# Loading a kernel's weights in three portions behind its first stage, and starting that stage before they are in

## The chip, the cores and the metric

The kernel runs on one core of a Trainium2 chip. The metric is the device time of one execution in microseconds (us). A core has a matrix engine (PE), a vector engine (DVE), an activation engine (ACT, also called ScalarE), a general engine (POOL) and SyncE (SP), which here only issues DMAs and waits. Each engine runs its own list of instructions in order; the lists meet at semaphores. DMAs are issued from ACT and from SP, and 16 DMA engines carry the bytes of both.

## The reference, cut to what matters

`x` has 8 batches of 512 tokens with 128 channels. Eight residual blocks follow each other, each on a layer norm of `x`:

```
x = x + attention_0(norm(x))      # 16 heads of width 8, allowed = block of query >= block of key, others score 0
x = x + fp4_ffn(norm(x))          # weights and activations quantised to 4 bits in blocks of 16
x = x + attention_1(norm(x))      # low-rank terms added to the weights, alibi bias, causal
x = x + ternary_ffn(norm(x))      # four 128..512 wide layers with scales
x = x + attention_2(norm(x))      # full
x = x + rwkv_ffn(norm(x)); x = x + ssm_block(norm(x)); x = x + expert_ffn(norm(x))
```

The first attention, all that the start of the program needs:

```
q, k, v = h @ Wq.T + bq, h @ Wk.T + bk, h @ Wv.T + bv      # h = norm(x)
s = q k' / sqrt(8);  s = 0 where a key's block of 32 comes after the query's
out = softmax(s) v @ Wo.T + bo
```

## The kernel before, in words

All of `x` stays on the core, in `X`, a batch being 512 columns. The stages (the attentions are stages 0, 2 and 4) run one after the other, and in each the 8 batches pass in frames, f = -1 to 8. Frame -1 prepares batches 0 and 1; frame f works on batch f, finishes f - 1 and prepares f + 1. A frame of an attention has 16 slots, s = 0 to 15 (`slots`), and each engine's list is written out by walking over frames and slots, so the code is the order.

**How a batch is prepared.** DVE takes the norm's statistics (`norm_stats`), POOL applies them (`norm_apply`, giving `xn`), PE turns `xn` (`transpose4`) and multiplies by Wq and Wk, ACT copies the results to `qf` and `kf`. Scores are wanted to more than bf16 precision, so `qf` and `kf` are each split into three bf16 parts (`qpart`, `kpart`, four operations; DVE does it for batch 0 of stage 0, POOL for later ones). SP writes the parts to DRAM (`part_out`: six DMAs for q, six for k) and reads them back in another arrangement (`stack`: two DMAs into `Qst`, two into `Kst`), six parts of 8 rows under each other for every head. The rows below the parts hold masks; `load_extra` loads them at the start of a stage, twelve DMAs in stage 0, and SP waits for them before it goes on. A last row of `Qst` is the negated maximum of the scores: PE forms the scores of a batch once to find the maxima (the matmul into banks 4 and 5, `scores`), DVE reduces them, the maxima are turned into `mT`, and SP copies `mT` into `Qst` (two DMAs at slot 6, two at slot 14). Only then are the scores formed transposed, exponentiated by ACT and multiplied by V.

The maxima of the next batch begin at slot 14 of a frame, so that batch's stacks must be in by then. SP's list in a frame: `part_out` of q at slot 5, `mT` at 6, `part_out` of k at 7, both stacks at 8, `mT` at 14. In frame -1 `part_out` of q and the q stack stand together at slot 5.

**How the program starts.** SP issues 8 loads of `X`. ACT issues `first_loads` (14: six constants, and the weights of stage 0's attention) and then `loads` (31, the weights of later stages), and then makes two small operands (`ident_b`, `bq_s`, which count `s_prepared` to 2). PE and DVE set the starting values of the semaphores, half each. `stage_starts` makes every engine, SP among them, wait at stage 0 for `X` of batch 0, POOL's fills, `first_loads` and `s_prepared`; from stage 1 on the engines wait for all of `loads`. The earliest reader of those is the quantiser of the fp4 weights, in frame 7 of stage 0, which has a wait of its own.

Of the kernel before, what the change touches and what calls it, by code (L numbers as in the profile page):

```python
# [143 lines left out]
class Attention(Stage):  # L144
# [161 lines left out]
    def tensor(self, pe):  # L306
        k = self.k
        k.stage_starts(pe, self)
        ps = k.ps

        def ready_t(b, g, tile):
# [108 lines left out]
        def misc_step(f, s):  # L420
# [43 lines left out]
            elif s == 9 and prev.valid():  # L464
# [2 lines left out]
                    pe.wait_ge(self.s_mT.sem, self.s_mT.at(f, 1))  # L467
                context_t(prev, 3)
            elif s == 10 and nxt.valid() and not (self.opened and f.c == -1):
                pe.wait_ge(self.s_cT_read.sem, self.s_cT_read.at(prev))  # L470
                pe.wait_ge(self.s_mT.sem, self.s_mT.at(f, 1))
                pe.wait_ge(self.s_k.sem, self.s_k.at(nxt))
                for t in range(NT):
                    mm = pe.matmul(misc[:, P * t:P * t + P], k.xnT[:, P * t:P * t + P], self.w["v"],
                                   start=True, stop=True)
                mm.then_inc(self.s_v_ps.sem, 1)
            elif s == 11 and prev.valid() and not full:
                pe.wait_ge(self.s_ctx.sem, self.s_ctx.at(prev))
                if nxt.valid():
                    pe.wait_ge(self.s_v.sem, self.s_v.at(nxt))  # L480
                transpose4(k.ctx_rows, self.s_c2_ps)
            elif s == 12 and prev.valid() and not full:
                pe.wait_ge(self.s_c2.sem, self.s_c2.at(prev))
                for t in range(NT):
                    mm = pe.matmul(misc[:, P * t:P * t + P], k.ctxT[:, P * t:P * t + P], self.w["o"],
                                   start=True, stop=True)
                mm.then_inc(self.s_o_ps.sem, 1)
            elif s == 13 and f.valid():
                if nxt.valid():
                    pe.wait_ge(self.s_v.sem, self.s_v.at(nxt))  # L490
                if full:
                    pe.wait_ge(self.s_ctx.sem, self.s_ctx.at(prev))
                else:
                    pe.wait_ge(self.s_x_done.sem, self.s_x_done.at(prev))
                context_t(f, 0)
            elif s == 15 and nxt.valid() and block:

                pe.wait_ge(self.s_mT.sem, self.s_mT.at(f))
                pe.wait_ge(self.s_v.sem, self.s_v.at(nxt))
                if not f.valid():  # L500
                    pe.wait_ge(self.s_k.sem, self.s_k.at(f.plus(2)))
                pe.matmul(misc, k.later[:, :], k.V[:, nxt.par, :, :, 0:DH], start=True, stop=False)
                for jt in range(1, NT):
                    mm = pe.matmul(misc[:, 0:P * jt], k.ones[:, :],
                                   k.V[:, nxt.par, jt, :, 0:DH].unsqueeze(1).broadcast_to([P, jt, H, DH]),
                                   start=False, stop=jt == NT - 1)
                mm.then_inc(self.s_vs_ps.sem, 1)
# [154 lines left out]
    def vector(self, dve):  # L662
        k = self.k
        k.stage_starts(dve, self)
        ps, misc = k.ps, k.ps[:, 7, :]

        def maxima(n, c):
# [70 lines left out]
        def frame(f):  # L738
            prev, nxt = f.plus(-1), f.plus(1)
            for s, _, _, (mb, c) in slots(f):  # L740
# [21 lines left out]
                if s == 9 and prev.valid():  # L762
                    context(prev, 3)
                if s == 10 and nxt.valid() and "bv" in self.w:
                    dve.wait_ge(self.s_v_ps.sem, self.s_v_ps.at(nxt))
                    dve.wait_ge(self.s_pv.sem, self.s_pv.at(nxt.plus(-2)))
                    out = k.V[:, nxt.par, :, :, 0:DH]
# [19 lines left out]
    def gpsimd(self, pool):  # L787
        k = self.k
        k.stage_starts(pool, self)

        def split(n, src, part, at):

# [45 lines left out]
        def frame(f):  # L838
# [25 lines left out]
                context(prev, 3)  # L864
            early(f, 3)
            if block and nxt.valid():
                v = "p (t c) -> p t c"
                x = xs_of(k.X, nxt).rearrange(v, t=NT)
                pool.wait_ge(self.s_cen.sem, self.s_cen.at(nxt))
# [13 lines left out]
    def sync(self, sp):  # L883
        k = self.k
        if self.opened:
            sp.wait_ge(self.s_x_done.sem, self.s_x_done.at(N(None, -1 - NB)))
        else:
            k.stage_starts(sp, self)
        k.load_extra(sp, self)

        def part_out(n, j):
# [29 lines left out]
        def frame(f):  # L921
            nxt = f.plus(1)
            for s in range(16):
                if s in (6, 14) and f.valid():
                    half = (s - 6) // 8
                    sp.wait_ge(self.s_mT.sem, self.s_mT.at(f, half + 1))
                    for a in range(2):
# [1 line left out]
                        sp.dma_start(k.Qst[r:r + 1, f.par, 4 * half:4 * half + 4, :]  # L929
                                     .rearrange("o i (t p) -> o (i t) p", t=NT),  # L930
                                     k.mT[16 * a:16 * a + 16, half, :]).then_inc(self.s_mrow.sem, 16)
                if s in (5, 7) and nxt.valid():
                    part_out(nxt, (s - 5) // 2)
                if s == (5 if f.c == -1 else 8) and nxt.valid():
                    stack(nxt, 0)
                if s == 8 and nxt.valid():
                    stack(nxt, 1)

        frames(sp, frame)


# [1666 lines left out]
class Kernel:  # L2608


    def __init__(self, nc, ctx, dram, out):
# [4 lines left out]
        self.s_fill = self.sem("fill")  # L2616
        self.s_prepared = self.sem("prepared")
        self.s_x_rest = self.sem("x_in_rest")
        self.s_first_weights = self.sem("first_weights")
        self.s_lora = self.sem("lora")  # L2620
        self.s_lora_full = self.sem("lora_full")
# [47 lines left out]
        self.ones = sb("ones", [P, P])  # L2669
        self.ps = ctx.enter_context(nc.psum_tensor("ps", [P, 8, T], F32))  # L2670
        self.scratch = nc.dram_tensor("parts_scratch", (2, 2, NKB, 64, T), BF16, kind="Internal").ap()
        self.first_loads, self.loads = [], []
        self.late_loads = []

        self.late_mem = [self.Qst[:, :, :, :].rearrange("p a h t -> p (a h t)").bitcast(F32),
# [50 lines left out]
    def late_weight(self, name):  # L2726
        src = self.dram[name]
        return self.late(list(src.shape), src)

    def load_late(self, sp, early):  # L2730
        for i, (dst, src) in enumerate(self.late_loads):
            sp.dma_start(dst, src).then_inc(self.s_late if i < early else self.s_later, 16)
# [28 lines left out]
    def const(self, name, dt):  # L2761
        src = self.dram["c_" + name]
        t = self.sb(name, list(src.shape), dt)
        self.first_loads.append((t[:], src))
        return t

    def weight(self, name, shape=None, src=None):

        src = self.dram[name] if src is None else src
        t = self.sb("w_" + name, list(src.shape) if shape is None else shape)  # L2770
        (self.first_loads if name[:4] in ("L0_W", "L0_b") else self.loads).append((t[:], src))
        return t

    def stage_starts(self, eng, st):

        if st.stage == FIRST_STAGE:
            eng.wait_ge(self.s_xin, 16)
            eng.wait_ge(self.s_fill, FILLS)
            eng.wait_ge(self.s_first_weights, 16 * len(self.first_loads))
            eng.wait_ge(self.s_prepared, 2)  # L2780
        else:
            eng.wait_ge(st.s_x_done.sem, st.s_x_done.at(N(None, -1)))
        if st.stage > 0:
            eng.wait_ge(self.s_weights, 16 * len(self.loads))

    def norm_of(self, n, st):

# [84 lines left out]
FILLS = 6  # L2872
# [3 lines left out]
def transformer(nc, dram, out):  # L2876
    with ExitStack() as ctx:
# [35 lines left out]

        @block.scalar
        def _(act):
            for dst, src in k.first_loads:
                act.dma_start(dst, src).then_inc(k.s_first_weights, 16)
            for dst, src in k.loads:
                act.dma_start(dst, src).then_inc(k.s_weights, 16)
            act.wait_ge(k.s_first_weights, 16 * len(k.first_loads))  # L2920
            act.activation(k.ident_b[:, :], k.ident[:, :], ACT.Copy).then_inc(k.s_prepared, 1)
            act.activation(k.bq_s[:, :], k.bq[:, :], ACT.Copy, scale=1.0 / math.sqrt(DH))\
               .then_inc(k.s_prepared, 1)
            for st in stages:
                st.scalar(act)

        @block.vector
        def _(dve):
            for sig in k.starts[1::2]:
                dve.sem_inc(sig.sem, sig.start)  # L2930
            for st in stages:
                st.vector(dve)
# [26 lines left out]
```

## Time and profile before

| | us |
|---|---|
| median of 3 executions | 2198.02 |
| lowest, highest | 2197.54, 2209.73 |
| the profiled execution, span of its instructions | 2200.8 |
| ACT has issued its 45 loads | 23.55 |
| first instruction of the first norm | 25.50 |
| first score matmul of batch 0 | 58.37 |
| slot 14 of frame 0, maxima of batch 1 begin | 99.94 |

For the profiled execution only the span is given, from the first to the last instruction; the median of the times is 2.8 us below it. PE is busy for 83% of the span, DVE 58%, ACT 47%, POOL 32%. In the profile a name like `SPq` or `ACTq` is an engine's instruction queue: its rows show when DMAs are issued, not when their data land. Times of rows are from the start of the span.

### The profile page before, as it was taken

What the parts mean: (1) busy time and instruction counts of PE and PEld (TensorE: products, weight loads), DVE (VectorE), ACT (ScalarE), POOL (GpSimd) and SP (SyncE); (2) the same over time, 40 slices, a digit from 0 to 9 for tenths busy, and PEclk for the clock granted to TensorE, in tenths of its full rate; (3) what the DMA queues carried; (4) which work ended last, traced back from release to release, by engine and by line L of the source; (5) the groups of instructions that cost most, each with busy time, mean ns of one, the idle gap of its engine ahead of it and who ended that gap; (6) DMA issues with size and microseconds to landing.
All of it is one profiled execution on the core that took longest, in us unless ns stands there. A gap on an engine that the chain in (4) does not pass through costs nothing.

```text
span 2200.8 us, 33255 instructions
## 1 busy us (share of the span) xinstructions
PE 1836.4 (83%) x11885; PEld 819.7 (37%) x11885; DVE 1287.4 (58%) x3442; ACT 1045.0 (47%) x1768; POOL 712.4 (32%) x796
## 2 busy tenths in 40 slices
PE   2788787765658888888999999899999957999998
PEld 0233233233433444444444444332332324444443
DVE  1666666627777767773100111598989916676663
ACT  1366556531213655565222322288888854445432
POOL 3166666454542322220100010122232115443330
PEclk9799999867877999998999999799999978999999
DMA  8323343000022343220000002233234110000000
GB/s 198 63 59 66 66 86 74 1 16 1 1 58 59 68 93 74 59 59 3 0 0 1 0 0 58 46 71 59 59 61 85 30 48 1 0 10 5 6 5 15
DMA packets 70269, 91.71 MB, mean 42 GB/s; under 512 B 13228, under 2 KB 63644, under 8 KB 65228
## 3 DMA queue, kind: packets, MB, share of 16 engines
q1 hardware_dynamic: 64680, 84.69, 18.7%
q10 hardware_dynamic: 5424, 4.89, 0.7%
q8 instruction: 95, 1.56, 0.3%
q14 instruction: 70, 0.57, 0.1%
HBM read 49.30 MB, written 39.85 MB: 41 GB/s over the span
## 4 chain that ended last, share of the span: by engine, by line
PE 51%; issue 7%; ACT 5%; DVE 4%; DMA 2%; SPq 1%; POOL 1%; DVEq 0%; ACTq 0%; POOLq 0%
PE ps L1402 9%; PE ps L410 5%; PE ps L2798 3%; PE ps L384 3%; PE ps L368 3%; PE ps L2079 2%; PE ps L396 2%; PE ps L2081 2%; PE ps L2097 2%; PE ps L352 2%; PE ps L330 2%; PE ps L1392 2%; DMA Qst<-mT 2%; PE ps L1772 1%; ACT Pr L579 1%
## 5 line engine op out<-in xcount | busy, mean ns | idle before, releaser
L686 DVE TENSOR_REDUCE mx<-ps 128x1 f32<-128x512 f32 (+3 forms) x1024 | 534.5, 583 | 156.2 <-PE ps L352 124.0
L586 ACT ACTIVATE Pr<-ps 128x1024 f32<-128x1024 f32 (+3 forms) x512 | 348.7, 706 | 229.6 <-PE ps L330 118.8
L579 ACT ACTIVATE Pr<-ps 128x512 f32<-128x512 f32 x512 | 274.6, 602 | 49.0 <-PE ps L384 43.7
L352 PE MATMUL ps<-Kst,Qst 63*128 63x512 bf16 (+3 forms) x1024 | 227.7, 329 | 66.7 <-DVE mx L686 25.6
L330 PE MATMUL ps<-Qst,Kst 64*128 64x512 bf16 (+3 forms) x1024 | 230.7, 328 | 56.0 <-issue 37.0
L682 DVE CUSTOM_DVE_ANT_0 vs<-ps,cT 128x512 f32<-128x512 f32 (+3 forms) x512 | 225.7, 487 | 84.8 <-PE ps L352 81.6
L368 PE MATMUL ps<-Pr,V 128*32 128x512 f32 (+3 forms) x2048 | 207.1, 479 | 4.6 <-ACT ctxU L592 2.9
L396 PE MATMUL ps<-Kst,Qst 63*128 63x512 bf16 x512 | 170.0, 403 | 6.6 <-DVE mx L686 4.4
L410 PE MATMUL ps<-Pr,V 128*32 128x256 f32 x2048 | 164.9, 394 | 8.4 <-ACT ctxU L592 7.5
L2826 POOL TENSOR_TENSOR ve<-mv,eps 128x4 f32<-128x4 f32 x41 | 8.7, 213 | 494.7 <-DVE mv L2815 494.7
L384 PE MATMUL ps<-Qst,Kst 64*128 64x512 bf16 x512 | 155.0, 388 | 15.4 <-issue 9.6
L1510 DVE SCALAR_TENSOR_TENSOR f_shared<-ps,w_L_s_w,f_own 128x512 f32<-128x512 f32 x32 | 23.4, 749 | 230.5 <-ACT f_own L1463 199.6
L352 PEld LDWEIGHTS ps<-Kst,Qst 63*128 63x128 bf16 x1024 | 68.8, 97 | 205.7 <-DVE mx L686 93.3
L330 PEld LDWEIGHTS ps<-Qst,Kst 64*128 64x128 bf16 x1024 | 72.7, 96 | 145.8 <-issue 76.3
L1402 PE MATMUL ps<-f_shared,w_L_h2T 128*128 128x512 f32 x256 | 113.0, 595 | 6.2 <-ACT f_shared L1456 6.2
L1402 PE MATMUL ps<-f_shared,w_L_h1T 128*128 128x512 f32 x256 | 112.2, 595 | 5.6 <-ACT xT L1468 4.8
L1537 POOL TENSOR_TENSOR X<-X,ctxU 128x512 f32<-128x512 f32 x8 | 10.1, 1266 | 309.4 <-DVE ctxU L1518 309.4
L828 POOL TENSOR_TENSOR rec<-dn,mone 128x16 f32<-128x16 f32 x32 | 93.0, 2905 | 0.0
L335 PE MATMUL ps<-tri_kq,ident_h 64*128 64x128 bf16 x512 | 85.5, 224 | 0.0
L333 PE MATMUL ps<-tri_kq,ident_h 64*128 64x128 bf16 x512 | 85.5, 224 | 0.0
L410 PEld LDWEIGHTS ps<-Pr,V 128*32 128x32 f32 x2048 | 40.7, 108 | 93.8 <-issue 72.8
L384 PEld LDWEIGHTS ps<-Qst,Kst 64*128 64x128 bf16 x512 | 32.0, 94 | 113.9 <-ACT Pr L579 70.7
(340 smaller groups left out, 3268.3 us busy)
## 6 DMA issues: line engine op xcount, KB each, us to landing
Qst<-parts_scratch SPq DMA_DIRECT2D x48, 384.0 KB, 6.0
Kst<-parts_scratch SPq DMA_DIRECT2D x48, 384.0 KB, 8.4
parts_scratch<-qpart SPq DMA_DIRECT2D x48, 192.0 KB, 2.7
parts_scratch<-kpart SPq DMA_DIRECT2D x48, 192.0 KB, 2.7
parts_scratch<-qpart SPq DMA_DIRECT2D x48, 128.0 KB, 2.6
parts_scratch<-kpart SPq DMA_DIRECT2D x48, 128.0 KB, 2.7
parts_scratch<-qpart SPq DMA_DIRECT2D x48, 64.0 KB, 2.3
parts_scratch<-kpart SPq DMA_DIRECT2D x48, 64.0 KB, 2.4
```

The source lines that it names most:

```text
L330: mm = pe.matmul(out, k.Kst[rows, b.par, 2 * q + tile, P * jt:P * jt + P], k.Qst[rows, b.par, 2 * q + tile, T - W:T], start=True, stop=not ...
L352: mm = pe.matmul(ps[:, 4 + a, lo:lo + W], k.Qst[rows, n.par, pair, P * it:P * it + P], k.Kst[rows, n.par, pair, 0:W], start=True, stop=True)
L368: mm = pe.matmul(ps[32 * a:32 * a + 32, 6, lo:hi], k.V[:, b.par, jt, 4 * q + a, :], k.Pr[:, g % 2, a, lo - (T - W):hi - (T - W)], start=jt ...
L384: pe.matmul(ps[:, self.bank_t(b, g, j), :], k.Kst[rows, b.par, 2 * q + tile, P * jt:P * jt + P], k.Qst[rows, b.par, 2 * q + tile, :], star ...
L396: pe.matmul(ps[:, self.bank_m(n, u), :], k.Qst[rows, n.par, pair, P * it:P * it + P], k.Kst[rows, n.par, pair, :], start=True, stop=True). ...
L410: mm = pe.matmul(ps[32 * a:32 * a + 32, 6, lo:hi], k.V[:, b.par, jt, 4 * q + a, :], k.Pr[:, g % 2, a, lo:hi], start=jt == 0 and half == 0, ...
L579: act.activation(k.Pr[:, g % 2, 2 * (j // 2) + 1 - j % 2, :], ps[:, self.bank_t(b, g, j), :], ACT.Exp).then_inc(self.s_exp.sem, 1)
L586: act.activation(k.Pr[:, g % 2, 2 * tile:2 * tile + 2, 0:W], ps[:, 2 * tile:2 * tile + 2, 0:W], ACT.Exp).then_inc(self.s_exp.sem, 1)
L682: dve.tensor_tensor_reduce(k.vs[:, at_u % 2, T - W:T], ps[:, bank, lo:lo + W], k.cT[:, 1, T - W:T], 1.0, -3e38, ALU.add, ALU.max, k.mx[:, ...
L686: dve.tensor_reduce(k.mx[:, half, at:at + 1], ps[:, bank, lo:lo + W], AX_X, ALU.max, negate=True).then_inc(self.s_max.sem, 1)
L828: pool.tensor_tensor(k.rec[:, :, :], k.dn2[:, :, :], k.mone[:, 0:1].unsqueeze(2).broadcast_to([P, NT, 4]), ALU.pow) .then_inc(self.s_part. ...
L1402: mm = pe.matmul(ps[:, at + m, :], w[:, kt, P * m:P * m + P], src[:, kt, :], start=kt == 0, stop=kt == self.KT - 1)
```

## The change

ACT issues 12 loads instead of 45. The first five (`start_loads`: `ident`, Wq, bq, Wk, bk of stage 0) count on a new semaphore; the next seven are what remains of `first_loads`. The other 33 (31, and two constants of stage 2, `tri_kq` and `ident_h`) are issued by SP in three portions, every third one of the list, after the stacks at slot 8 of frames 0, 1 and 2. SP no longer waits before `load_extra`. The common wait at the start of stage 0 is gone: DVE waits for batch 0's `X`, PE for `start_loads`, POOL for its fills, and the wait for the rest of `first_loads` (`prepared`) stands in front of V's projection (PE), V's bias (DVE) and the first use of `bo` (POOL). In frame -1 of every attention `part_out` of k moves from slot 7 to slot 5, ahead of the q stack. ACT takes over half of the semaphore starts that DVE set.

```diff
@@ Attention.tensor / vector / gpsimd
         k.stage_starts(pe, self)
+        if not self.opened:
+            pe.wait_ge(k.s_start_weights, 16 * len(k.start_loads))
...
+                if f.c == -1:
+                    k.prepared(pe)
...
         k.stage_starts(dve, self)
+        if not self.opened:
+            dve.wait_ge(k.s_xin, 16)
...
         k.stage_starts(pool, self)
+        if not self.opened:
+            pool.wait_ge(k.s_fill, FILLS)
...
@@ Attention.sync
             sp.wait_ge(self.s_x_done.sem, self.s_x_done.at(N(None, -1 - NB)))
-        else:
-            k.stage_starts(sp, self)
         k.load_extra(sp, self)
...
-                if s in (5, 7) and nxt.valid():
-                    part_out(nxt, (s - 5) // 2)
+                if s == 5 and nxt.valid():
+                    part_out(nxt, 0)
+                if s == (5 if f.c == -1 else 7) and nxt.valid():
+                    part_out(nxt, 1)
                 if s == (5 if f.c == -1 else 8) and nxt.valid():
                     stack(nxt, 0)
                 if s == 8 and nxt.valid():
                     stack(nxt, 1)
+                if s == 8 and not self.opened and 0 <= f.c < 3:
+                    k.load_weights(sp, f.c)
...
+    def load_weights(self, sp, third):
+
+        for dst, src in self.loads[third::3]:
+            sp.dma_start(dst, src).then_inc(self.s_weights, 16)
...
+    def prepared(self, eng):
+
+        eng.wait_ge(self.s_fill, FILLS)
+        eng.wait_ge(self.s_first_weights, 16 * len(self.first_loads))
+        eng.wait_ge(self.s_prepared, 2)
...
@@ the scalar engine's start
+            for dst, src in k.start_loads:
+                act.dma_start(dst, src).then_inc(k.s_start_weights, 16)
+            for sig in k.starts[1::4]:
+                act.sem_inc(sig.sem, sig.start)
             for dst, src in k.first_loads:
                 act.dma_start(dst, src).then_inc(k.s_first_weights, 16)
-            for dst, src in k.loads:
-                act.dma_start(dst, src).then_inc(k.s_weights, 16)
-            act.wait_ge(k.s_first_weights, 16 * len(k.first_loads))
+            act.wait_ge(k.s_start_weights, 16 * len(k.start_loads))
```

How it moves instructions, at two places on SP. The first is frame -1 of stage 0, batch 0's parts going out to DRAM (`parts_scratch`) and coming back as stacks. Before:

```order
L900 DMA parts_scratch<-qpart 64x2x512
L900 DMA parts_scratch<-qpart 64x512
L917 DMA Qst<-parts_scratch 48x4096 [waits attention_scores_t,attention_q_out]
L917 DMA Qst<-parts_scratch 48x4096
L905 DMA parts_scratch<-kpart 64x3x512 [waits attention_split]
L905 DMA parts_scratch<-kpart 64x2x512
L905 DMA parts_scratch<-kpart 64x512
```

and now:

```order
L910 DMA parts_scratch<-qpart 64x512
L915 DMA parts_scratch<-kpart 64x3x512 [waits attention_split]
L915 DMA parts_scratch<-kpart 64x2x512
L915 DMA parts_scratch<-kpart 64x512
L927 DMA Qst<-parts_scratch 48x4096 [waits attention_scores_t,attention_q_out]
L927 DMA Qst<-parts_scratch 48x4096
L927 DMA Kst<-parts_scratch 48x4096 [waits attention_k_out]
```

The q stack no longer waits between the two groups of writes; both stacks are read one behind the other. The second place is frame 0, from batch 1's K stack to the copy of batch 0's maxima (`mT`) at slot 14, as it is now:

```order
L927 DMA Kst<-parts_scratch 48x4096 [waits attention_k_out]
L927 DMA Kst<-parts_scratch 48x4096
L2748 DMA tri_kq<-in_c_tri_kq 128x256
L2748 DMA w_L_Bq<-in_L_Bq 8x128
L2748 DMA w_L_fp_w<-in_L_fp_w 128x1152
L2748 DMA w_L_h1T<-in_L_h1T 128x2048
L2748 DMA w_L_mu_k<-in_L_mu_k 128x1
L939 DMA Qst<-mT 1x16x128 [waits attention_mT]
L939 DMA Qst<-mT 1x16x128
```

Five of the 11 loads of this portion are shown; before, `mT` followed the K stack directly. Frames 1 and 2 have 10 each at the same place (`h2T` is in frame 1, `w2T` and `w3T` in frame 2).

## Rows read from the trace of the kernel before

**Rows 1.** The page's head: span, and busy time and share of each engine.

```profile
span 2200.8 us, 33255 instructions
PE 1836.4 (83%) x11885; PEld 819.7 (37%) x11885; DVE 1287.4 (58%) x3442; ACT 1045.0 (47%) x1768; POOL 712.4 (32%) x796
```

**Rows 2.** Timeline from the start: start, duration, engine, line, operation; idle before, releaser.

```profile
23.08 0.47 ACTq L2919 DMA_DIRECT2D w_L_mu_k<-in_L_mu_k  x1
...
25.50 0.88 DVE L2810 BATCH_NORM_STATS2 bn<-X 128x6 f32<-128x128 f32 x4 [25.50 <-ACT bq_s L2922]
26.41 0.38 DVE L2815 BATCH_NORM_AGGREGATE mv<-bn 128x2 f32<-128x6 f32 x4
...
29.20 1.04 POOL L2838 TENSOR_TENSOR xn<-cen,rstd 128x512 f32<-128x512 f32 x1
```

**Rows 3.** Timeline of SP's queue: writing and reading of batch 0's parts.

```profile
37.57 3.98 SPq L900 DMA_DIRECT2D parts_scratch<-qpart  x6
43.25 0.81 SPq L917 DMA_DIRECT2D Qst<-parts_scratch  x2
44.10 4.42 SPq L905 DMA_DIRECT2D parts_scratch<-kpart  x6
```

**Rows 4.** Timeline: batch 0's K stack and the first score matmul.

```profile
51.82 0.77 SPq L917 DMA_DIRECT2D Kst<-parts_scratch  x2
...
58.37 0.61 PE L352 MATMUL ps<-Kst,Qst 63*128 63x512 bf16 x2 [10.43 <-DMA Kst<-parts_scratch]
```

**Rows 5.** Stretches: length, busy time per engine, PEclk, DMA share, GB/s.

```profile
4.00:12.00 8.00, 0.00 (x0) 0.00 (x0) 0.00 (x0) 0.00 (x0) 0.72 (x6) 1.00 1.07 279
...
28.00:34.00 6.00, 2.76 (x6) 1.22 (x6) 0.38 (x4) 0.60 (x1) 5.28 (x7) 1.00 1.05 116
```

**Rows 6.** DMAs issued up to 70 us: KB of each, us to landing.

```profile
Kst<-in_c_mask_k SPq DMA_DIRECT2D x4, 120.0 KB
w_L_WkT<-in_L_WkT ACTq DMA_DIRECT2D x3, 64.0 KB, 5.6
```

**Rows 7.** Everything on X up to 60 us: landing times of its loads.

```profile
DMA to landing us min/median/max: 3.5/5.8/7.7
```

**Rows 8.** Frames 0 and 1: stacks of the next batch, PE at slot 14.

```profile
86.37 0.77 SPq L917 DMA_DIRECT2D Kst<-parts_scratch  x2
...
99.94 0.42 PE L352 MATMUL ps<-Kst,Qst 63*128 63x512 bf16 x2
...
135.31 0.79 SPq L917 DMA_DIRECT2D Qst<-parts_scratch  x2
...
136.54 0.77 SPq L917 DMA_DIRECT2D Kst<-parts_scratch  x2
...
147.03 0.39 PE L352 MATMUL ps<-Kst,Qst 63*128 63x512 bf16 x2 [1.28 <-DMA Kst<-parts_scratch]
```

**Rows 9.** Stretches around frame 1's K stack and in the weight loads (columns as above).

```profile
143.00:145.00 2.00, 1.85 (x15) 0.47 (x13) 1.93 (x6) 1.28 (x3) 0.00 (x0) 1.00 0.93 160
...
16.00:20.00 4.00, 0.00 (x0) 0.00 (x0) 0.00 (x0) 0.00 (x0) 0.00 (x0) 1.00 0.96 325
```

**Rows 10.** Frame 1: `mT` at slot 14, and PE's first use of it.

```profile
148.86 1.19 SPq L929 DMA_DIRECT2D Qst<-mT  x2
...
152.94 0.39 PE L330 MATMUL ps<-Qst,Kst 64*128 64x512 bf16 x2
```

**Rows 11.** PE idle at frame 1's slot 8, and PE's clock behind it.

```profile
128.24 0.61 PE L330 MATMUL ps<-Qst,Kst 64*128 64x512 bf16 x2 [3.02 <-issue]
...
128.00:134.00 6.00, 5.76 (x33) 1.31 (x34) 3.00 (x7) 3.42 (x5) 3.24 (x5) 0.50 0.28 64
```

**Rows 12.** Stage 2: the opening K stack and the first scores.

```profile
653.38 0.78 SPq L917 DMA_DIRECT2D Kst<-parts_scratch  x2
...
664.78 0.39 PE L352 MATMUL ps<-Kst,Qst 63*128 63x512 bf16 x2
```

**Rows 13.** The longest event of a semaphore on PE, from the rows of line 2877.

```profile
L2877 PEldq EVENT_SEMAPHORE  x1: 51/51/51, 2200.8 to 2200.8; - x1
```

More of the change, by code:

```diff
@@ L764, in frame @@
                 if s == 10 and nxt.valid() and "bv" in self.w:
+                    if f.c == -1:
+                        k.prepared(dve)
                     dve.wait_ge(self.s_v_ps.sem, self.s_v_ps.at(nxt))
@@ L866, in frame @@
             if block and nxt.valid():
+                if f.c == -1:
+                    k.prepared(pool)
                 v = "p (t c) -> p t c"
@@ L2618, in __init__ @@
         self.s_x_rest = self.sem("x_in_rest")
+        self.s_start_weights = self.sem("start_weights")
         self.s_first_weights = self.sem("first_weights")
@@ L2671, in __init__ @@
         self.scratch = nc.dram_tensor("parts_scratch", (2, 2, NKB, 64, T), BF16, kind="Internal").ap()
-        self.first_loads, self.loads = [], []
+        self.start_loads, self.first_loads, self.loads = [], [], []
         self.late_loads = []
@@ L2763, in const @@
         t = self.sb(name, list(src.shape), dt)
-        self.first_loads.append((t[:], src))
+        loads = self.start_loads if name == "ident" else \
+            self.loads if name in ("tri_kq", "ident_h") else self.first_loads
+        loads.append((t[:], src))
         return t
@@ L2770, in weight @@
         t = self.sb("w_" + name, list(src.shape) if shape is None else shape)
-        (self.first_loads if name[:4] in ("L0_W", "L0_b") else self.loads).append((t[:], src))
+        if name in ("L0_WqT", "L0_bq", "L0_WkT", "L0_bk"):
+            self.start_loads.append((t[:], src))
+        else:
+            (self.first_loads if name[:4] in ("L0_W", "L0_b") else self.loads).append((t[:], src))
         return t
     def stage_starts(self, eng, st):
[L2776 to L2781, printed above, removed]
+        if st.stage > FIRST_STAGE:
             eng.wait_ge(st.s_x_done.sem, st.s_x_done.at(N(None, -1)))
-        if st.stage > 0:
             eng.wait_ge(self.s_weights, 16 * len(self.loads))
+    def prepared(self, eng):
+        eng.wait_ge(self.s_fill, FILLS)
+        eng.wait_ge(self.s_first_weights, 16 * len(self.first_loads))
+        eng.wait_ge(self.s_prepared, 2)
     def norm_of(self, n, st):
@@ L2923, in _ @@
                .then_inc(k.s_prepared, 1)
+            act.wait_ge(k.s_prepared, 2)
             for st in stages:
@@ L2928, in _ @@
         def _(dve):
-            for sig in k.starts[1::2]:
+            for sig in k.starts[3::4]:
                 dve.sem_inc(sig.sem, sig.start)
```

## The prediction, made before the changed kernel ran

> **What bounds the kernel now.** I read the page's head first [rows 1]: PE is busy for 83% of the span, so in the steady part only PE's work counts, and the change touches none of it. What it can win lies where PE has nothing to do, at the start. I then read the timeline from zero [rows 2]. ACT issues loads until 23.55 us; only behind them come its two small operands, and everybody waits for these: DVE starts the first norm at 25.50. The work from there to the parts of q takes 12 us, up to SP's first write at 37.57 [rows 3]. Then comes a chain through DRAM on SP: q parts out (3.98), 1.7 of waiting for them, q stack, k parts out (4.42), 3.3 of waiting, K stack at 51.82, and PE's first score at 58.37 [rows 3, 4]. All later work hangs on that first score. So the question is at what time it comes in the changed kernel, and what the 33 loads cost at their new places.
>
> **Part 1: the engines start at first use.** Nothing needs the long list of loads any more. SP issues X from the start, and the fastest load landed in 3.5 [rows 7]: 4.2. Statistics take 1.3 (25.50 to 26.79, two groups of DVE), POOL ends `xn` at 30.24, so 3.4 more [rows 2]: 9.0. The five start loads are issued by about 3.2 and land at most 5.6 later [rows 6], at 8.8, so they don't bind. From `xn` to the first write of q parts it was 37.57 - 30.24 = 7.3 [rows 2, 3]: 16.3. DVE has a wait in between, for all of X: the last load is issued by 7.1 and lands at the latest 7.7 on [rows 7], 14.8, and behind it come 1.3 of statistics and 2.4 of splitting: 18.5 at the latest. I take 17.3. The seven other first loads are issued by about 7 and are wanted for V, about 8 us later; that costs nothing. Semaphore starts: there are fewer than 160, PE sets half. The trace of before hides them. From below they cost nothing; from above 80 at the 51 ns of the one such row [rows 13] are 4.1 us, done at 4.8, hidden under X and the norm; I take nothing. ACT has a quarter, between its loads, and is idle then.
>
> **Part 2: the masks become the late ones.** SP no longer waits before `load_extra`, so its twelve DMAs follow the loads of X at once, from 7.1 to about 14. But before it sends q parts, SP waits until they have landed. They were hidden before (issued from 25.4, needed at 37.57). Now I must ask how fast they land. The DMA engines are full from 4 to 12 us, share 1.07 at 279 GB/s [rows 5]. X and 12 first loads are 8 x 256 KB (512 x 128 floats) and 8 x 64 KB [rows 6] and some small ones, 2.63 MB: 9.4 us, from 2.3 to 11.7. The masks are 4 x (120 + 120 + 8) KB, 1.02 MB, in small pieces, and while they had the engines for themselves these were full at only 116 GB/s [rows 5]: 8.8 us, to 20.5. The DMA work of frame 1's stacks ends near 144.9 (from 143 to 145 the share is 0.93) and PE goes at 147.03 [rows 8, 9]: some 2 us from last data to release. So SP goes on at **22.5**, not at 17.3. From below, if masks moved as fast as stacks did at the end of frame 1 (160 GB/s, [rows 9]), 20.1; from above 24.5, if both groups hinder each other for 2 us. I take 22.5, since the row for it is of the masks themselves.
>
> **Part 3: k parts ahead of the q stack.** From 22.5: q parts 3.98, k parts 4.42 [rows 3] (`kpart` is ready 2.9 after `qpart`, in time), so the q stack is issued at 31.0 and the K stack as soon as the k parts are in DRAM, 1.7 later by the wait behind the q parts. Both stacks now travel together, as in frame 1, where PE was released 147.03 - 135.31 = 11.7 after the q stack's issue [rows 8]. First score at 31.0 + 11.7 = **42.7**. In the old order it would be 22.5 + (58.37 - 37.57) = 43.3: the reordering alone is worth 0.6 us, because what it takes out of SP's list it gives back as two stacks sharing the engines. In stages 2 and 4 the same move is worth nothing: there the K stack was issued at 653.38 for a first score at 664.78 that stands behind PE's own work [rows 12], while batch 0's took 6.5. In stage 4 no wait of PE for a stack is seen at all.
>
> **Part 4: 33 loads in SP's list.** They are issued in 0.45 to 0.5 each as on ACT [rows 2], 5.5 us in frame 0 and 5 in frames 1 and 2. SP is free there for 11.5 us and more (in frame 1 from 137.3 to 148.9 [rows 8, 10]), so nothing queues behind them. Their bytes: 1.85 MB in frame 0 (`h1T`, 128 x 2048 floats, is the largest), 1.59 in frame 1, 0.92 in frame 2. At 325 GB/s [rows 9] these are 5.7, 4.9 and 2.8 us. They stand in the same queue behind the K stack, on which PE waits in frame 1 already [rows 8]. I take it that the stack isn't slowed, and that the weights come through at 144.9 + 4.9 = 149.8. The `mT` copy at slot 14 is issued at 148.86, its second half at 149.5, and PE uses it at 152.94 [rows 10]: it loses at most some tenths. In frame 0 the stack's data end near 94.9 by the same distances (86.37 + 10.5 - 2 [rows 8]) and PE wants `mT` only at 99.94 + 5.9 = 105.8 (as in frame 1, 152.94 - 147.03) [rows 8, 10]; frame 2 has the fewest bytes. Cost: 0, from above 16 (rival C).
>
> The Trainium skill's page "DMA: Bandwidth & Descriptors", section "Queues, rings and completion order", speaks against this part: the increment of a DMA's semaphore lands only after every earlier write of that DMA engine, whatever queue it was on. By that rule `mT` cannot be reported before the weights ahead of it are in: the sum stays 2182 while the weights are fast, and becomes rival D's time if they are slow. No row of before shows a small copy behind a large load, so the trace neither agrees nor contradicts.
>
> **The sum.** 58.37 - 42.7 = 15.7 us. The profiled span of 2200.8 [rows 1] becomes 2185.1. The median of the runs lies 2.8 below the span; **2198.0 - 15.7 = 2182**. That everything after the first score moves by the same amount rests on the list being the same; PE's slow clock in the opening follows the pattern of its work, which does not change.
>
> **The rivals.** *A, masks bind, weights free*: 2182, give or take 3. 58%.
> *B, the masks are in in time.* For it: their issue ends at 14, and packets of two kinds may share the engines better than I add them. Against: the 116 GB/s at a full share. Then 17.3 + 8.4 + 11.7 = 37.4, gain 21.0: 2177. 20%.
> *C, the weights slow the K stacks.* If DMA engines serve the loads along with the stacks, the stack of frame 1 is late by up to 4.9, of frame 2 by 2.8, of frame 0 by 5.7 less the 3 us it had in hand (released about 96.9, wanted at 99.94 [rows 8]): 10.4 together. A longer wait can also drop PE's clock: after an idle of 3.02 us it stood at 0.50 of full speed (1.2 instead of 2.4 GHz) for 6 us [rows 11], at most 3 us of loss each time, twice: 6. Gain 15.7 less 6 to 16.4: 2188 to 2198, most likely 2190. 14%.
> *D, slower: `mT` stuck behind the weights.* If these came at the masks' 116 GB/s, the portions would take 16, 13.7 and 7.9 us; in frame 0 `mT` would land at 94.9 + 16 + 2 = 112.9 instead of 105.8 (7.1 late), in frame 1 at 160.6 instead of 152.9 (7.7), in frame 2, placed like frame 1 but with 7.9 for 13.7, 1.9 late. With a clock drop of 3 each it is 26: 2208, slower than before. The loss passes the gain of 15.7 where the loads come at less than about 150 GB/s: 8 us late and three drops. Against it: these loads have long rows and had 325 GB/s. 4%.
> *E, anything else*, such as a start that some unseen wait holds where it was: 2198. 4%.
>
> **Chances and range.** A measurement of this kernel tells 1% (22 us) from no change. A, C and E stay within 1%. B lies at 2177, 1 us short of it, so about a third of B and a little of A pass 2176: faster 0.10. Slower than 2220 would take more than D: 0.02. Same 0.88. The range runs from below B (2175) through most of C (2194).
>
> **What would show it.** *Part 1*: DVE's first norm near 5, `xn` near 9, ACT's loads ended by 8. *Part 2*: SP's first write of q parts at 20 to 24.5, and its wait put down to the masks; B if at 16 to 18.5. *Part 3*: first score at 42.7, 20 us after that write. *Part 4*: PE's wait for the K stack in frame 1 still 1 to 2 us, no wait for `mT` at slot 0 of frames 1 to 3; from frame 3 on every row earlier by the same 15 to 16 us. I am wrong if the first score comes at its time and the later frames give it back, or if SP writes q parts long before or after 22.5.

## The result

| | before | changed |
|---|---|---|
| median of the times beside the first comparison (4 executions each) | 2201.70 | 2178.36 |
| median in a second comparison (11 and 6 executions) | 2200.68 | 2179.28 |
| span of the profiled execution | 2200.8 | 2176.9 |
| the same, second profile of each kernel | 2195.1 | 2179.8 |
| first score matmul, first and second profile | 58.37, 58.55 | 40.98, 40.65 |

The ratio is 0.9893, 95% interval 0.9872 to 0.9914, in the first comparison and 0.9903 (0.9887 to 0.9919) in the second: 23.5 us (19 to 28) and 21.3 us (18 to 25) less. The forecast was 2182, range 2175 to 2194, taken from a median of before of 2198.0; with a fourth execution that median is 2201.70. The gain sits at 1% almost exactly, so whether it is "faster by over 1%" or "within 1%" is not decided by these runs.

### The profile page after: what moved, and what is told of

It is laid out like the page before. It is cut to its first block, busy times and chain, and to the rows that moved or that the text cites. A ratio compares the mean times of both kernels' runs of the same rounds, so it can differ in the third digit from the quotient of the medians.

```text
span 2176.9 us, 33252 instructions
## 1 busy us (share of the span) xinstructions
PE 1834.5 (84%) x11885; PEld 818.5 (38%) x11885; DVE 1288.3 (59%) x3442; ACT 1045.8 (48%) x1768; POOL 712.1 (33%) x796
## 3 DMA queue, kind: packets, MB, share of 16 engines
q1 hardware_dynamic: 68376, 89.05, 19.7%
## 4 chain that ended last, share of the span: by engine, by line
PE 52%; issue 7%; ACT 5%; DVE 4%; DMA 2%; SPq 1%; POOL 1%; DVEq 0%; ACTq 0%; POOLq 0%
PE ps L1416 9%; PE ps L412 5%; PE ps L2823 3%; PE ps L386 3%; PE ps L370 3%; PE ps L2093 2%; PE ps L398 2%; PE ps L2095 2%; PE ps L2111 2%; PE ps L354 2%; PE ps L332 2%; PE ps L1406 2%; DMA Qst<-mT 2%; ACT Pr L583 1%; PE ps L1786 1%
## 5 line engine op out<-in xcount | busy, mean ns | idle before, releaser
L354 PE MATMUL ps<-Kst,Qst 63*128 63x128 bf16 (+3 forms) x1024 | 228.3, 330 | 65.1 <-DVE mx L692 26.5
L1551 POOL TENSOR_TENSOR X<-X,ctxU 128x512 f32<-128x512 f32 x8 | 10.1, 1267 | 309.4 <-DVE ctxU L1532 309.4
```

The lines of the kernel that those rows point to most:

```text
L354: mm = pe.matmul(ps[:, 4 + a, lo:lo + W], k.Qst[rows, n.par, pair, P * it:P * it + P], k.Kst[rows, n.par, pair, 0:W], start=True, stop=True)
```

## The profile after

The first lines of the start, by the timeline (start in us, length, engine, line, operation, operands, count, and in brackets the idle time before it with what ended it):

```profile
2.65 0.45 ACTq L2942 DMA_DIRECT2D w_L_WkT<-in_L_WkT  x1
4.16 0.88 DVE L2835 BATCH_NORM_STATS2 bn<-X 128x6 f32<-128x128 f32 x4 [4.16 <-DMA X<-in_x]
...
5.60 0.40 ACTq L2946 DMA_DIRECT2D later<-in_c_later  x1
...
6.56 1.04 SPq L2892 DMA_DIRECT2D Kst<-in_c_mask_k  x1
...
7.84 1.04 POOL L2863 TENSOR_TENSOR xn<-cen,rstd 128x512 f32<-128x512 f32 x1
...
11.18 1.09 PE L2823 MATMUL ps<-ident,xn 128*128 128x128 f32 x4 [11.18 <-issue]
...
12.45 0.87 DVE L2835 BATCH_NORM_STATS2 bn<-X 128x6 f32<-128x128 f32 x4 [7.00 <-DMA X<-in_x]
...
13.26 0.64 SPq L2892 DMA_DIRECT2D Kst<-in_c_onoff  x1
...
18.20 0.69 DVE L703 TENSOR_TENSOR qpart<-rest,qpart 128x512 bf16<-128x512 f32 x1
```

These answer to [rows 2]. The norm starts at 4.16 and `xn` is ready at 8.88. Then something is odd: PE starts at 11.18, 2.3 us later, and its idle time is put down to "issue", to nothing that this view shows. The last load it needs, `WkT`, was issued at 2.65 and landed at 7.9. What stands before PE's first matmul in its list is its share of the semaphore starts. The rows of that line, in the changed kernel and in the one before (how often, ns of one as min/median/max, first and last start in us):

```profile
L2965 PEldq EVENT_SEMAPHORE  x67: 51/51/51, 0.8 to 10.9; - x67
L2937 PEldq EVENT_SEMAPHORE  x67: 51/51/51, 0.8 to 10.9; - x67
```

So PE sets 67 starting values, one each 0.15 us, until 11.0, although each row lasts only 51 ns. ACT's 34, a quarter of all, fill its gap from 3.1 to 5.60, at 0.07 us each.

Then SP's chain and the first score, the answer to [rows 3, 4], and SP's waits up to 31 us (us in total, times, longest):

```profile
21.29 3.95 SPq L910 DMA_DIRECT2D parts_scratch<-qpart  x6
25.28 3.89 SPq L915 DMA_DIRECT2D parts_scratch<-kpart  x6
29.27 0.99 SPq L927 DMA_DIRECT2D Qst<-parts_scratch  x2
31.44 0.77 SPq L927 DMA_DIRECT2D Kst<-parts_scratch  x2
...
40.98 0.61 PE L354 MATMUL ps<-Kst,Qst 63*128 63x512 bf16 x2 [12.07 <-DMA Kst<-parts_scratch]
```

```profile
SPq L905 <- DVE qpart L703: 5.0, 1, 5.0
SPq L910 <- DMA Kst<-in_c_onoff: 2.3, 1, 2.3
```

`qpart` is ready at 18.89, but SP then waits 2.3 us more for the last mask. The masks are the last to come, as rival A had it. The stretches show how fast they travelled (length, busy time of PE, PEld, DVE, ACT, POOL, granted clock, DMA share, GB/s); compare [rows 5]:

```profile
4.00:12.00 8.00, 0.82 (x4) 0.72 (x4) 1.26 (x8) 1.69 (x3) 3.92 (x10) 1.00 1.13 276
12.00:14.00 2.00, 1.26 (x3) 0.50 (x2) 1.25 (x8) 0.60 (x1) 0.19 (x2) 1.00 1.14 139
14.00:16.00 2.00, 1.22 (x3) 0.15 (x1) 0.17 (x1) 0.69 (x1) 1.98 (x3) 1.00 1.10 144
16.00:18.00 2.00, 1.93 (x2) 0.35 (x2) 1.93 (x3) 0.03 (x1) 1.10 (x1) 1.00 1.08 144
18.00:20.00 2.00, 1.20 (x5) 1.23 (x6) 1.84 (x4) 0.66 (x1) 0.00 (x0) 1.00 0.56 76
20.00:22.00 2.00, 0.85 (x4) 0.56 (x3) 1.93 (x7) 0.00 (x0) 0.00 (x0) 1.00 0.01 4
```

The DMA engines are full until about 19, and SP goes on at 21.3, some 2 us later.

In the frames the portions lie where the diff puts them. In frame 0 the first and the last load of the portion and `mT` behind them, the stretches there, and the waits of PE for the stacks in frames 1 to 3 (compare [rows 8, 9, 10]):

```profile
70.07 0.42 SPq L2748 DMA_DIRECT2D tri_kq<-in_c_tri_kq  x1
...
74.35 0.43 SPq L2748 DMA_DIRECT2D w_L_mu_k<-in_L_mu_k  x1
84.67 1.20 SPq L939 DMA_DIRECT2D Qst<-mT  x2
```

```profile
80.00:82.00 2.00, 1.80 (x15) 0.37 (x12) 1.24 (x4) 1.37 (x3) 0.00 (x0) 1.00 1.04 424
82.00:84.00 2.00, 2.00 (x20) 0.88 (x18) 1.86 (x7) 1.91 (x4) 0.53 (x2) 1.00 0.74 240
84.00:86.00 2.00, 1.84 (x22) 0.58 (x18) 1.94 (x6) 1.20 (x5) 2.00 (x2) 1.00 0.01 2
```

```profile
PE ps L354 <- DMA Kst<-parts_scratch: 2.9, 2, 1.5
```

Before, the same view reads:

```profile
PE ps L352 <- DMA Kst<-parts_scratch: 6.1, 3, 2.6
```

So the portion of frame 0 is through at 83.5, 1.2 us before `mT` is issued, and the wait for the K stack did not grow, it shrank.

In frame 1 the portion is still moving when `mT` goes out. SP's row, the stretch, and the weight load of PE that uses `mT`:

```profile
130.76 1.20 SPq L939 DMA_DIRECT2D Qst<-mT  x2
130.00:132.00 2.00, 1.88 (x22) 0.58 (x18) 1.85 (x6) 1.13 (x5) 2.00 (x2) 1.00 0.95 351
134.83 0.10 PEld L332 LDWEIGHTS ps<-Qst,Kst 64*128 64x128 bf16 x2 [0.55 <-DMA Qst<-mT]
```

This copy took up to 3.0 us to land and PE's weight load waited 0.55 us for it. In frames 0 to 3 of both profiles of before no copy of `mT` took over 1.9 us. In the eight profiles with three portions the longest took 2.2 to 3.7 us, and five of these show a wait for it, of 0.5 to 0.8 us.

## The experiments

Every kernel below was run in a comparison with the kernel before (medians 2200.68 to 2200.70). "First score" is the start of PE's first score matmul in its own profile, 58.37 before.

### The old order in the opening

```diff
-                if s == (5 if f.c == -1 else 7) and nxt.valid():
+                if s == 7 and nxt.valid():
                     part_out(nxt, 1)
```

> The changed kernel, with the old order in frame -1: q stack ahead of the k parts. It tells what the reordering alone is worth. By my sum (0.6 us) the first score comes at about 41.6 instead of 40.98; the first q parts are still written at 21.3. Rival: the reordering saves the whole wait for the q parts (20.8 us from first q part to first score before, 19.7 now), so the first score comes at 42.1, and if stages 2 and 4 profit too, 2 to 6 us are lost there. What follows the first score takes 2136 to 2142 us by the first theory, as in the two kernels so far; by the second at least 2 more than in the changed kernel, 2138 or more in every run.

Measured: 2182.04, ratio 0.9919 (0.9894 to 0.9944), first score 42.81:

```profile
21.62 3.98 SPq L910 DMA_DIRECT2D parts_scratch<-qpart  x6
27.39 0.81 SPq L927 DMA_DIRECT2D Qst<-parts_scratch  x2
28.24 4.35 SPq L915 DMA_DIRECT2D parts_scratch<-kpart  x6
35.88 0.77 SPq L927 DMA_DIRECT2D Kst<-parts_scratch  x2
...
42.81 0.61 PE L354 MATMUL ps<-Kst,Qst 63*128 63x512 bf16 x2 [13.95 <-DMA Kst<-parts_scratch]
```

From the write of the q parts to the first score it is 21.2 us here, and 19.7 and 19.5 in the two profiles of the changed kernel: the reordering is worth 1.5 to 1.7 us on this stretch, too little for the medians to tell. Over all profiles, the four with the old order take 20.8 to 21.2 us and six with the new order 19.2 to 19.7 us; the two with both edits below take 19.8 and 20.6. In the changed kernel the K stack is issued 4.4 us sooner than here, but takes 9.5 us to its use instead of 6.9; it then travels beside the q stack. From the first score to the end it is 2134.3 us here, less than in the changed kernel, so nothing speaks for the rival that stages 2 and 4 profit too.

### Fewer semaphore starts on PE

33 of the 67 increments with which PE sets starting values go to SP, behind its mask loads (the expectation says 35 of 69).

```diff
+        if at.stage == FIRST_STAGE:
+            for sig in self.starts[68::2]:
+                sp.sem_inc(sig.sem, sig.start)
...
-            for sig in k.starts[0::2]:
+            for sig in k.starts[0:68:2]:
```

> The changed kernel; of the 69 semaphore starts that PE sets, 35 of later stages go to SP, behind its mask loads. In the changed kernel PE's first matmul stands at 11.14, with xn ready at 8.88 and the last start weight landed at 7.85, and waits for nothing that is seen. Theory: the starts take 0.15 us each on PE, 10.4 us together, three times the 51 ns that I took as upper bound. Then PE's first matmul comes at 8.9 to 9.0 and qf 2.2 us sooner. Rival: something else holds PE until 11.1 (a weight that lands late), and nothing moves. By the theory that masks bind, the first write of q parts stays at 21.3 and the time is that of the changed kernel; if the masks do not bind, it comes at about 17 to 19 and the time falls by 2.

Measured: 2179.67, ratio 0.9904 (0.9877 to 0.9930), first score 39.74. PE's increments and its first matmul:

```profile
L2968 PEldq EVENT_SEMAPHORE  x34: 51/51/51, 0.8 to 5.9; - x34
...
8.97 1.09 PE L2823 MATMUL ps<-ident,xn 128*128 128x128 f32 x4 [8.97 <-POOL xn L2863]
```

```profile
SPq L910 <- DMA Kst<-in_c_onoff: 2.8, 1, 2.8
SPq L905 <- DVE qpart L703: 1.4, 1, 1.4
```

PE is through with its increments at 5.9 and starts as soon as `xn` is there, 2.2 us sooner, and "issue" has turned into a named releaser: the increments were what held it. But SP's wait for the masks takes up half of it, and the q parts are written at 20.22 instead of 21.29. Neither of the two cases expected (no change, or 17 to 19) came: the masks themselves landed 1.1 us sooner, at 20.2, and why is open.

### Half of the masks behind batch 0's K stack

Of the twelve mask loads the six of the second buffer are issued when batch 0's stacks have been.

```diff
-        k.load_extra(sp, self)
+        k.load_extra(sp, self, (0, 1) if self.opened else (0,))
...
+                if s == 8 and not self.opened and f.c == -1:
+                    k.load_extra(sp, self, (1,))
```

> The changed kernel; of the 12 mask loads only the 6 for batch 0's half of the buffers stand at the start, the other 6 follow batch 0's K stack. If the masks bind, SP is released at about 17 to 18 and goes on to wait for qpart, ready at 18.9: first write at 19.0 instead of 21.29, first score at 38.7, 2.3 us gained. If they don't bind, nothing moves. The 6 later ones are awaited by SP behind the K stack, about 39 to 42, which may cost up to 2 us if they hinder the K stack.

Measured: 2178.61, ratio 0.9899 (0.9875 to 0.9922), first score 39.49. Of SP's two waits at this place one is left:

```profile
SPq L905 <- DVE qpart L703: 8.7, 1, 8.7
```

The masks are in at 17.5, as expected. The q parts go at 19.84, 1.45 us sooner (2.3 were expected), and now `qpart` itself is the last to come, at 19.8 instead of 18.9. Two of DVE's operations on it took 0.7 to 0.9 us more than usual here, one in the changed kernel.

### Both

The two edits together, run twice.

> Both edits together: 6 masks later and half of PE's semaphore starts on SP. The two limits lie one behind the other, so together they should give more than the sum of each alone (2.3 and 0): first write of q parts at about 17, first score at 36.7, 4 us sooner than in the changed kernel, about 2174. If one of the theories is false it gives what the other gives alone.

> The version with 35 of TensorE's semaphore starts on SyncE and half of the masks loaded behind batch 0's K stack, unchanged, beside the changed kernel on the same chip. Theory: its first score, 2.0 us earlier (38.94), shows in the medians: 1 to 3 us under the changed kernel, which stays inside the scatter of a handful of runs. Rival (the start is no longer all that counts): no difference, or slower.

Measured: 2178.25, ratio 0.9902 (0.9877 to 0.9927), and 2175.42, ratio 0.9893 (0.9876 to 0.9911); q parts at 18.31 and 17.58, first score at 38.94 and 37.33. The second time the changed kernel ran on the same chip, with 2179.28. At the q parts the two edits bring 3.0 and 3.6 us, more than the sum of each alone (1.1 and 1.45), as two bounds one behind the other should, but less than the 4 expected. At the first score it is 2.0 and 3.3 us. The medians lie 3.9 us apart in the second comparison, more than the 1 to 3 of the theory; in the first no changed kernel ran beside it. The intervals overlap, so this is the best version of the study by its profile, and not shown to be faster by its times. From the K stack's issue to its use it took 10.4 and 10.0 us with both edits, 9.7 with the halved masks alone, and 9.5 to 9.9 in kernels without masks behind it, so a cost of these masks is not shown.

### All 33 loads in frame 0

```diff
-                if s == 8 and not self.opened and 0 <= f.c < 3:
+                if s == 8 and not self.opened and f.c == 0:
                     k.load_weights(sp, f.c)
...
-        for dst, src in self.loads[third::3]:
+        for dst, src in self.loads:
```

> The change, but with all 33 loads issued by SyncE behind the K stack of frame 0, none in frames 1 and 2. Theory (rivals C and D, a transfer in the way): the weights are 4.26 MB, about 13 us at the 325 GB/s of the busiest slice before, so they reach from 70 to past 85, where mT (84.67 us in the trace of the change) and batch 1's first part of the stacks are wanted: mT's landing, and the stack reads of the next frame, come some us late, PE waits there for a DMA, and the time is 2181 to 2186. Rival (my prediction: they cost nothing off the start): no new wait over 1 us on a DMA in frame 0 or 1, the time stays at 2178 within 3 us, and the three portions were not needed.

Measured: 2184.10, ratio 0.9943 (0.9923 to 0.9963), inside the 2181 to 2186 expected, first score at 40.80 as in the changed kernel. So what is lost is lost later: some 5 us by the medians, 9 to 11 by the ratios. (The loads are 4.36 MB together.) First SP's queue, then a stretch, then PE:

```profile
81.78 3.17 SPq L2748 DMA_DIRECT2D w_L_WkfT<-in_L_WkfT  x1
...
87.40 1.19 SPq L939 DMA_DIRECT2D Qst<-mT  x2
```

```profile
88.00:90.00 2.00, 0.08 (x1) 0.00 (x0) 0.00 (x0) 0.60 (x1) 0.00 (x0) 1.00 1.02 242
90.00:92.00 2.00, 0.00 (x0) 0.00 (x0) 0.00 (x0) 0.00 (x0) 0.00 (x0) 1.00 0.10 19
92.00:94.00 2.00, 1.36 (x6) 0.28 (x6) 0.29 (x1) 0.72 (x1) 0.00 (x0) 0.59 0.00 0
```

```profile
92.64 0.61 PE L332 MATMUL ps<-Qst,Kst 64*128 64x512 bf16 x2 [4.56 <-DMA Qst<-mT]
```

Two things delay `mT`: SP's own list (a load's issue took 3.17 us, so `mT` is issued at 87.40 instead of 84.67), and the bytes ahead of it, which move until about 90; PE is released some 2 us behind them, 5.2 us after the issue. The copies took 4.2 to 4.6 us to land, where they take 1.8 in frame 0 of the changed kernel. And behind the wait PE's clock is granted at 0.59 on average in the next stretch. This is rival D's mechanism, and it exists; the three portions keep the change clear of all but half a microsecond of it. The experiment can't tell whether the small copy's own bytes came late, queued behind the large ones, or only the report of its end did.

### The 33 loads on ACT, all the rest of the change kept

```diff
+            for dst, src in k.loads:
+                act.dma_start(dst, src).then_inc(k.s_weights, 16)
...
-                if s == 8 and not self.opened and 0 <= f.c < 3:
-                    k.load_weights(sp, f.c)
```

> The change, but the 33 loads are issued by ScalarE at the start, behind its seven other early loads; SyncE issues none. Theory (the deferral of the loads is most of the gain): 33 loads at about 0.45 us put ScalarE's first compute from 10.4 to about 25, the eviction of the transposed normed features behind it; the q parts are written at about 34, the first score starts at 53 to 55 us in place of 40.98, and some 13 of the 17.4 us at the first score are lost: 2190 to 2193. Rival (the waits at first use alone bring it, the portions little): first score within 3 us of 41, time 2178.

Measured: 2197.37, ratio 0.9985 (0.9968 to 1.0001), first score 59.12, later than before.

```profile
20.99 3.43 ACTq L2946 DMA_DIRECT2D w_L_s_h<-in_L_s_h  x2
...
34.02 0.60 ACT L621 ACTIVATE xnT<-ps 128x512 f32<-128x512 f32 x1
```

PE has its transpose ready at 12.3 and waits 22.40 us for ACT. I had expected ACT at 25 and the q parts at 34; its loads were all issued at 32.29 and the q parts came at 39.92, since from 20.99 on a load took up to 2.24 us to issue and a group of two 3.43. The direction held, the size was off: the waits at first use and the new order bring nothing at the first score while ACT is the engine that issues the loads.

### The portions alone, common waits and old order kept

```diff
 (the kernel before, and in it)
+                if s == 8 and not self.opened and 0 <= f.c < 3:
+                    k.load_weights(sp, f.c)
...
-            for dst, src in k.loads:
-                act.dma_start(dst, src).then_inc(k.s_weights, 16)
```

> The kernel before with one part of the change alone: SyncE issues 31 loads in frames 0 to 2, but all engines still wait together for the first loads, the features, the fills and the prepared operands, and the order of frame -1 is the old one. Theory: ScalarE has 14 loads to issue, to about 8.5 us, the common start comes at 10 to 11; the masks are then issued behind it, so the q parts are written at about 22.5 to 25, and the first score starts at 43 to 46 (old order): 12 to 15 of the 17.4 us at the first score, 2180 to 2186. Rival (the early start of each engine is worth most of it): first score at 50 or later, 2188 or more.

Measured: 2187.88, ratio 0.9948 (0.9931 to 0.9965), first score 47.47. That is 10.9 us of the 17.4, less than the 12 to 15 expected, and between the two theories.

```profile
7.90 0.65 ACTq L2923 DMA_DIRECT2D w_L_WoT<-in_L_WoT  x1
...
13.56 0.31 ACT L2925 ACTIVATE ident_b<-ident 128x128 bf16<-128x128 f32 x1 [3.70 <-DMA w_L_WoT<-in_L_WoT]
...
14.19 0.87 DVE L2816 BATCH_NORM_STATS2 bn<-X 128x6 f32<-128x128 f32 x4 [14.19 <-ACT bq_s L2926]
```

I had counted the issuing of the loads, but the common wait is for their landing: `WoT`, the last of fourteen, is there 5.7 us after its issue. The start moves from 25.50 to 14.19 (11.3). Here the masks are no bound: SP's one long wait at the q parts (5.4 us) is for `qpart`, as before.

### Both kernels once more

> The kernel before, unchanged, for further profiles and times of it. In the trace of before the time from the first score to the end is 2142.5 us, in that of the change 2136.0. Theory (that part is chance from run to run, the gain is what stands at the first score): this trace gives 2134 to 2139. Rival (the shifted start saves some 6 us further on in every run): 2142 to 2144 again. The ratio to before is 1.000 within its interval.

> The changed kernel, unchanged, for more times and a second profile. Its first median stood 23.5 us under before (interval 19 to 28), its first score 17.4 earlier. Theory (the gain is the start's 17.4 and the first frames' shorter waits for the K stack, 1 to 4 us): over more runs the difference is 18 to 22 us, the first score is at 41.0 again, and the time from it to the end is within 2 us of 2136. Rival (something of 5 us and more lies further on that the start does not show): the difference stays at 23 or more.

Measured: before 2203.06 (12 executions), ratio to its own earlier form 1.0007 (0.9992 to 1.0022), changed 2179.28, 0.9903. From the first score to the end it is 2142.5 and 2136.5 us in the two profiles of before, 2136.0 and 2139.2 in those of the change. In the second pair the order is the other way round, so the 6.5 us by which the first pair differed behind the first score are chance. The second profile of the change missed my "within 2 us of 2136" by 1.2.

## Why the prediction was right, step by step

The likeliest case (A) came out, and the mechanism with it: the first score came 17.4 us sooner for 15.7 forecast. That the time came within 4 us of 2182 is in part luck: the gain was 6 to 8 us larger than forecast, and the median of before from which I subtracted was 3.7 us lower than the one it was then compared with.

**Part 1** held for the norm (4.16 against "near 5") and `xn` (8.88 against 9.0). It failed on the semaphore starts. I bounded them from above by 51 ns each [rows 13] and called them hidden; 67 of them hold PE until 11.0, which is 0.15 us each. The row I had was of one event at the very end of the program (2200.8 us), and its 51 ns are the length of the row, not the distance from one to the next. Nor does the trace of before hide them: its rows of line 2937, shown above, have the same 67 up to 10.9, under the common start at 25.50. They cost 2.2 us at PE and stayed mostly hidden, not for my reason but because the masks were later still: without them (33 starts moved) the q parts went only 1.1 us sooner. `qpart` was ready at 18.9 and not at 17.3. From `xn` to `qpart` it was 10.0 us instead of the 7.3 of before; the 2.2 us at PE and 0.7 of a slow operation of DVE make up the difference. Starts and masks are two bounds 1 to 2 us apart, and taking away either shows the other. The 5.6 us that I took as the most a start load needs are a median in [rows 6]; the last was in by 7.9, so nothing hung on it.

**Part 2** had the mechanism right and the rate wrong. SP wrote the q parts at 21.3, not 22.5. The 1.02 MB of masks went at 139 to 144 GB/s rather than 116 [rows 5]: 11.7 + 1.02 MB / 140 GB/s + 2 is 21.0. The row I took was of masks, but not at that place. What came lies midway between my value and the bound from below (20.1).

**Part 3** undersized the reordering: 1.5 to 1.7 us for 0.6. I had taken the 11.7 us from the q stack's issue to PE's release of frame 1 [rows 8], and that held (29.27 to 40.98 is 11.7). What was off were the two ends: the q stack is issued 8.0 us behind the q parts, not 8.5, and the old order would have needed 21.2, not 20.8.

**Part 4**, cost 0, held to within the tenths that it allowed `mT` in frame 1: there PE's weight load waited 0.55 us, and none in the second profile. The waits for the K stack went from 6.1 to 2.9 us in all (5.3 and 2.0 in the second profiles). So rival C is out for the change, and D's mechanism costs it half a microsecond at most; it showed in full when all loads came at once. The Trainium skill's page "DMA: Bandwidth & Descriptors", section "Queues, rings and completion order", says that an increment follows all earlier writes of its DMA engine: in the changed kernel nothing was ahead of `mT` in frame 0 and it landed in 1.8 us; in frame 1 weights were ahead of it and it took up to 3.0; and in the kernel with all loads in frame 0 `mT` released PE some 2 us after the last byte of the weights. All three agree with that rule, though none tells it from a plain queue. It was right to let it count only as a rival, weighed by bytes and rate.

**The sum** was 15.7, the first score gave 17.4 and the times 21 to 23.5. The masks are 1.2 of the difference at the first score, the chain behind the q parts 0.5. For what is left, this table sets the gain at the first score beside that of the times, and PE's waits for DMAs between the first score and 245 us (before: 6.1, second profile 5.3):

| kernel | gain at first score | waits | gain by the ratio, interval |
|---|---|---|---|
| changed | 17.4 | 2.9 | 23.5 (19 to 28) |
| changed, again | 17.7 | 2.0 | 21.3 (18 to 25) |
| old order | 15.6 | 4.1 | 17.8 (12 to 23) |
| PE's starts moved | 18.6 | 3.5 | 21.1 (15 to 27) |
| masks halved | 18.9 | 4.0 | 22.2 (17 to 28) |
| both | 19.4 | 5.8 | 21.6 (16 to 27) |
| both, again | 21.0 | 3.0 | 23.5 (20 to 27) |
| all loads in frame 0 | 17.6 | 8.9 | 12.5 (8 to 17) |
| loads on ACT | -0.8 | 2.4 | 3.3 (0 to 7) |
| portions alone | 10.9 | 3.5 | 11.4 (8 to 15) |

Gain at the first score plus 5.7 (the mean of before) less the waits lies within every interval: 20.2 and 21.4 for the changed kernel, 14.4 for all loads at once, 2.6 for the loads on ACT. So the shorter waits, some 3 us, may be the home of what the start does not show. That is an argument from a table, made afterwards; no run isolates it, and why PE meets its K stack later there stays open: from issue to use the stack took 10.0 us in frame 2 of the change and 10.1 before, so it is not the stack that got faster.

My sign "from frame 3 on every row earlier by the same 15 to 16 us" did not hold. The first copy of `mT` comes 17.1 us earlier in the change (62.36 for 79.47), the one at 682.36, in stage 2, 20.2, and the last pair of stage 4, at 1763.40, 22.1. But the second profile of before has that last pair at 1756.85, 6.6 us from its twin. So one profile of each kernel can't place what lies behind the start.

**How the gain divides** at the first score: deferring the loads alone 10.9, the waits at first use with the new order alone -0.8, both 17.4. The two parts are one after the other on the same path: waits at first use are worth nothing while ACT still issues for 23 us and more, and take 6.5 us off with the new order once it does not, of which 4.7 come without the new order (47.47 to 42.81).

## What to carry to other kernels

When a long list of loads goes away from the front, look for the next thing that the list covered: here the landing of the last load that is still waited for in common, then the masks and a run of semaphore increments, the last two within 2 us of each other. A kernel's early loads can go behind its first stage in portions at hardly any cost, if each portion's bytes are through before the next small DMA on which an engine waits; work that out with the rate of the stretch. For a run of small instructions take the distance from the first to the last row, not the length of one. And several engines waiting together for loads pay for the last landing, not for the last issue.

## What the hardware showed that I had not expected

- A run of semaphore increments at the start took 0.15 us each on PE (67 by 11.0 us, rows of 51 ns), 0.09 us on DVE (33 from 0.8 to 3.7) and 0.07 us on ACT (34 from 3.1 to 5.5). Moving 33 of PE's freed it at 5.9 and brought its first matmul 2.2 us sooner.
- Issuing a DMA is not a fixed 0.45 us: one took 3.17 us (SP, all loads in frame 0), and a group of two 3.43 us (ACT, 33 loads there), and everything behind them in that list waited. Each time the 16 DMA engines were full, but they were nearly as full (share 0.96, [rows 9]) from 16 to 20 us of before, where the issues took 0.45 to 0.6; what else it takes is open.
- One or two DVE operations on the parts took 0.7 to 0.9 us more than their like where POOL normed the next batch at the same time, and which ones changed from profile to profile (the subtraction here, the cast behind it in the second profile, 1.16 for 0.43). In the two profiles of before and the two kernels in which POOL was done by then, none did. That is a coincidence in time in every profile, and no run changes it alone. The same subtraction of 128x512, with POOL at work on X and without:

```profile
16.30 1.41 DVE L699 TENSOR_TENSOR rest<-qf,qpart 128x512 f32<-128x512 f32 x1
...
19.44 0.69 DVE L699 TENSOR_TENSOR rest<-kf,kpart 128x512 f32<-128x512 f32 x1
```
